# Shifted rows for the FFN moved tile by tile into two buffers, in a six-layer attention kernel

## What is computed

```python
def shift_tokens(t):
    a, s = jnp.split(t, 2, -1)
    s = jnp.pad(s, ((0, 0), (1, 0), (0, 0)))[:, :-1]
    return jnp.concatenate([a, s], -1)
...
def ffn_layer(x, g, bln, W1, b1, W2, b2):
    mu = x.mean(-1, keepdims=True)
    var = ((x - mu) ** 2).mean(-1, keepdims=True)
    xn = (x - mu) / jnp.sqrt(var + 1e-05) * g + bln
    hg = xn @ W1 + b1
    a, gate = jnp.split(hg, 2, -1)
    return a * jax.nn.gelu(gate, approximate=False) @ W2 + b2
...
for i in range(DEPTH):
    x = attn_layer(shift_tokens(x), Wqkv[i], q_scale[i], k_scale[i], Wo[i]) + x
    x = ffn_layer(shift_tokens(x), ln_g[i], ln_b[i], W1[i], b1[i], W2[i], b2[i]) + x
```

## Time and profile before

| | |
|---|---|
| median of 3 runs | 2215.2 us (2207.94 to 2216.47) |
| the profiled execution | 2216.56 us |
| its span in the trace | 2214.5 us |
| busy: TensorE / VectorE / ScalarE / GpSimd | 86% / 69% / 58% / 66% of the span |
| mean granted TensorE clock | 0.938 |
| transfers into `behind` | 48 instructions, 24 of line 218 and 24 of line 219 |

### The profile page before, as it was taken

The page is one execution under the profiler, slowest core; times in us unless marked ns, Lnnn a source line. Parts: engine busy times, 40 slices in busy tenths (PEclk is TensorE's granted clock), DMA queues, the critical chain, the costliest instruction groups (busy, mean ns, idle before and its releaser), DMA issues.

```text
span 2214.5 us, 61533 instructions
## 1 busy us (share of the span) xinstructions
PE 1898.6 (86%) x24771; PEld 1306.2 (59%) x24771; DVE 1528.6 (69%) x2364; ACT 1293.0 (58%) x1860; POOL 1472.5 (66%) x2112
## 2 busy tenths in 40 slices
PE   5789999968789988899889888898889888898885
PEld 2455555545566666566666566566666666566663
DVE  2445454458777787787777867787677876787872
ACT  3567777535556655565656655565556655565552
POOL 3344444458778677787777867787677776787771
PEclk8899999988999999999999999999899998999998
DMA  4999999920020000110000200002000020000000
GB/s 122 307 349 355 340 360 345 323 58 9 11 60 11 11 13 11 47 23 11 12 11 21 52 11 12 11 10 62 10 11 13 10 61 11 12 10 12 13 9 22
DMA packets 109618, 175.05 MB, mean 79 GB/s; under 512 B 49517, under 2 KB 72985, under 8 KB 108569
## 3 DMA queue, kind: packets, MB, share of 16 engines
q1 hardware_dynamic: 109336, 171.11, 24.9%
HBM read 87.06 MB, written 68.29 MB: 70 GB/s over the span
## 4 chain that ended last, share of the span: by engine, by line
PE 33%; DVE 17%; issue 11%; DMA 11%; POOL 4%; ACT 2%; SPq 1%; DVEq 0%; POOLq 0%; ACTq 0%
DMA behind<-x 10%; DVE turned L703 7%; PE yps L610 6%; PE ring L594 6%; PE ring L629 6%; PE ring L580 5%; PE ring L535 4%; PE ring L545 4%; DVE rsum L739 2%; DVE smax L724 2%; DVE pT L752 2%; DVE ss L718 1%; ACT squares L378 1%; POOL roped L328 1%; DVE stats L768 1%
## 5 line engine op out<-in xcount | busy, mean ns | idle before, releaser
L703 DVE TENSOR_TENSOR turned<-ring,ropes 128x1024 f32<-128x1024 f32 x384 | 447.5, 1207 | 20.4 <-PE ring L535 19.8
L610 PEld LDWEIGHTS yps<-wvo,oT 128*128 128x128 f32 x3072 | 398.4, 207 | 53.2 <-issue 50.0
L610 PE MATMUL yps<-wvo,oT 128*128 128x128 f32 x3072 | 405.6, 289 | 2.8 <-issue 2.1
L535 PE MATMUL ring<-wqk,xT 128*128 128x512 f32 x768 | 368.2, 602 | 7.7 <-issue 3.7
L328 POOL TENSOR_TENSOR roped<-roped,rnorm 128x1024 f32<-128x1024 f32 x192 | 362.3, 1902 | 7.5
L244 POOL TENSOR_TENSOR roped<-turned 128x512 f32<-128x512 f32 x288 | 357.5, 1271 | 13.3 <-DVE turned L703 13.3
L378 ACT ACTIVATE squares<-ring 128x1024 f32<-128x1024 f32 x192 | 197.5, 1029 | 268.8 <-DVE turned L703 268.0
L545 PE MATMUL ring<-ident,roped 128*128 128x128 f32 x1536 | 218.6, 292 | 146.0 <-ACT squares L378 128.7
L1233 POOL TENSOR_SCALAR less<-less,lowest 128x512 f32<-128x512 f32 x256 | 174.4, 693 | 241.1 <-DVE lowest L1202 241.1
L545 PEld LDWEIGHTS ring<-ident,roped 128*128 128x128 f32 x1536 | 187.9, 151 | 224.3 <-POOL roped L328 159.8
L1202 DVE CUSTOM_DVE_ANT_0 less<-ps_b,shifted 128x512 f32<-128x512 f32 x256 | 166.6, 689 | 222.4 <-PE ps_b L1065 80.0
(11 more groups left out here) (136 smaller groups left out, 3017.4 us busy)
## 6 DMA issues: line engine op xcount, KB each, us to landing
shifted<-scratch_w SPq DMA_DIRECT2D x64, 1024.0 KB, 12.7
scratch_w<-wrows SPq DMA_DIRECT2D x48, 1026.0 KB, 11.0
scratch_w<-x SPq DMA_DIRECT2D x16, 1026.0 KB, 10.3
wqk<-in_l_wqkv SPq DMA_DIRECT2D x6, 1024.0 KB, 5.4
xs<-xs SPq DMA_DIRECT2D x96, 48.0 KB, 1.9
wv<-in_l_wqkv SPq DMA_DIRECT2D x6, 512.0 KB
wo<-in_l_wo SPq DMA_DIRECT2D x24, 128.0 KB
xs<-x SPq DMA_DIRECT2D x96, 32.0 KB
```

Source lines behind the costliest of these rows:

```text
L535: last = nc.tensor.matmul(out[:, half, :], xT[:, t % SEQT * P:(t % SEQT + 1) * P], wqk[:, layer_of(t), at + half * 512:at + (half + 1) * 5 ...
L610: last = nc.tensor.matmul(out[:, 0:D], oT[:, h, :], wvo[:, layer_of(t), r, j, :], start=h == 0, stop=h == HEADS - 1)
L703: ins = nc.vector.tensor_tensor(turned[:, n, part, :].rearrange("p (h d) -> p h d", d=DH), heads, table, ALU.mult)
```

## The change

The four tiles of a group are moved one by one. In step `n`, after `windows(n)`, SyncE now issues the transfers of tile `n - 3`: first the single row that comes from the tile before (not for a group's first tile), then, behind `y_added` of this very tile, the 127 rows. `behind` has two buffers, used by the groups in turn, and the guard against overwriting it looks one group further back. The statistics wait for 7 transfers per group instead of 2.

```diff
-        behind = sb("behind", [P, SEQT, D // 2])
+        behind = sb("behind", [P, 2, SEQT, D // 2])
...
-        OWN, PREV, LOADS, BEHIND = 3 * 16, 2 * 16, 10 * 16, 2 * 16
+        OWN, PREV, LOADS, BEHIND = 3 * 16, 2 * 16, 10 * 16, (2 * SEQT - 1) * 16
...
-            return x[:, g % BATCH * SEQT + tile, 0:half], behind[:, tile, :]
+            return x[:, g % BATCH * SEQT + tile, 0:half], behind[:, g % 2, tile, :]
...
-            def shift(g):
-
-                at, half = g % BATCH * SEQT, D // 2
-                sp.wait_ge(s["y_added"], SEQT * (g + 1))
-                at_least(sp, s["xn_made"], g)
-                sp.dma_start(behind[1:P, :, :], x[0:P - 1, at:at + SEQT, half:D]).then_inc(s["behind_in"], 16)
-                sp.dma_start(behind[0:1, 1:SEQT, :], x[P - 1:P, at:at + SEQT - 1, half:D]).then_inc(s["behind_in"], 16)
+            def shift(t):
+
+                if live(t):
+                    at, tile, half, p = t % TILES, t % SEQT, D // 2, t // SEQT % 2
+                    at_least(sp, s["xn_made"], t // SEQT - 1)
+                    if tile > 0:
+                        sp.dma_start(behind[0:1, p, tile, :], x[P - 1:P, at - 1, half:D]).then_inc(s["behind_in"], 16)
+                    sp.wait_ge(s["y_added"], t + 1)
+                    sp.dma_start(behind[1:P, p, tile, :], x[0:P - 1, at, half:D]).then_inc(s["behind_in"], 16)
...
                 windows(n)
-                if n % SEQT == 2 and n >= SEQT:
-                    shift(n // SEQT - 1)
+                shift(n - 3)
                 if n % (SEQT * BATCH) == 10 and n // (SEQT * BATCH) + 1 < DEPTH:
                     load_layer(n // (SEQT * BATCH) + 1)
-            for g in range(GROUPS - 1, GROUPS):
-                shift(g)
+            for t in range(NT - 3, NT):
+                shift(t)
...
-            nc.gpsimd.memset(behind[0:1, 0, :], 0.0).then_inc(s["cleared"], 1)
+            nc.gpsimd.memset(behind[0:1, :, 0, :], 0.0).then_inc(s["cleared"], 1)
```

## The result

| | before | changed |
|---|---|---|
| median of the runs | 2214.12 us (2207.94 to 2216.47) | 2025.36 us (2022.62 to 2026.38) |
| the profiled execution | 2216.56 us | 2026.38 us |
| its span in the trace | 2214.5 us | 2024.3 us |
| mean granted TensorE clock | 0.938 | 0.974 |

The ratio is 0.9149, 95% interval [0.9128, 0.9171]. The change is faster by 189 us; 165 were forecast (2049 us), and the range ended at 2032. The way and the mechanism were forecast, the size was not: 24 us more came out.

What follows compares the result with a forecast made beforehand. Bound: VectorE's wait before `stats` for the transfer into `behind`, stalling all engines. Plain stretches 140.5, value-weight stretches 24.8 and last group 6.6, less 4.6 new waits, give 167.3 us; 2216.56 becomes 2049 us, range 2032 to 2088.

Steps and rivals of the forecast that it cites:

- What bounds the kernel: VectorE's wait before `stats` for the transfer into `behind`, 171.9 us in total, with TensorE and GpSimd idle and TensorE's clock lowered.
- the late tile: Fourth tile's 127 rows, issued after its own `add_y`, land within 3.68 us; at most 0.75 of 7.46 us wait stays.
- VectorE's wait: Sign: the wait before `stats`, once per group, falls from 171.9 us in total to under 25.
- SyncE's 7 us: Sign: the 7.00 us that the second transfer instruction held SyncE behind the 508-row one are gone.
- TensorE's wait for the squares: Sign: TensorE's idle time until ScalarE's squares let it turn q, 5.93 us in one stretch, is nearly gone.
- The plain stretches: 18 stretches from one `smax` to the next, 423.09 us together, shrink to 15.7 each; gain 140.5 us.
- The five stretches with value weights: Stretches where the next layer's value weights are multiplied, 128.33 us together, shrink to 20.7 each; gain 24.8 us.
- The new waits: Thin margins on VectorE, TensorE and GpSimd cost 0.2 us for each of 23 stretches, 4.6 us in total.
- the fixed time: Rival: a transfer's time is fixed, so 127 rows come as late as 508 and nothing changes; 2217 us, 3%.
- The transfer that lands later than the windows' copy: Rival: the fourth tile's copy meets others on the queue and takes 5.5 us; 31 us less gain, 2080 us, 9%.
- SyncE as the bound: Rival: added instructions each hold the queue 7.00 us, making a SyncE step 19.4 us; slower, 2450 us, 2%.
- The rule weighed against the change: Skill page's general DMA cost: 127 KB lands 2.3 us after issue, 31.75 KB 2.07, so splitting gains 0.2 us a group.

Runs made afterwards that it cites:

- the pairs: Changed kernel, but tiles moved two at a time, 254 rows behind every second tile's add_y; 2073.72 us, ratio 0.9377.
- the cut at 112: Changed kernel with each 127-row copy into `behind` cut into 112 and 15 partitions; 2020.39 us in the first set, 2016.84 in the second.

## Why the prediction was too small

*What bounds the kernel, and the late tile:* right. VectorE's wait fell to 18.4 us (under 25 expected), the transfer landed after 3.74 us (3.68), SyncE's 7 us are gone, and TensorE's wait for the squares fell from 128.7 us to 3.0.

*The plain stretches:* right, 139.95 us against 140.5. The reason given for 15.7 us was half wrong. I had TensorE as their bound; TensorE idles 0.45 us there (15.52 less 15.07 in the stretch above) while VectorE stands 0.83 us, and the pairs show that each further microsecond of VectorE's wait is felt in full. With the cut at 112 the 18 stretches sum to 275.97 us, 0.4 us less each, and there TensorE is the bound. VectorE's work and wait together (14.59 and 0.83) come within half a microsecond of TensorE's 15.07, so 15.7 fits either bound; that the number held is in part luck.

*The five stretches with value weights:* this is the step that failed: "TensorE idles 3.55 before the turns and loses 3.02 − 1.95 = 1.07 to the clock: 20.63 stay". The loss to the clock was read on one group of instructions only. The value weights' products between the two, 3.78 us at 1.2 GHz and 2.06 at 2.4, lost another 1.72. With it 18.91 stay; measured were 18.47 to 18.90. The term is 35.35 us, not 24.8. The trace of before held the price only at the low clock, 3.55 to 3.79 us in all five places, and I took it for the work's own. It could have told that this is the price at 1.2 GHz: ahead of the first layer the same products took 3.79 us in a stretch with a granted clock of 0.50:

```profile
473.18 3.79 PE L566 MATMUL ring<-wo,wvT 64*128 64x128 f32 x32 [0.98 <-ACT wvT L437]
...
472.90:478.00 5.10, 4.82 (x34) 4.13 (x35) 0.00 (x0) 2.56 (x6) 0.00 (x0) 0.50 0.09 21
```

A stretch with a granted clock of 0.86 should have been searched for every instruction in it, and these products given bounds of half the time, 1.89 us, and 3.78.

*The new waits, 4.6 us:* they did not come. The plain stretches' 15.7 held with the remaining wait in it.

*The five stretches ahead of those, 7.2 us:* not forecast. They contain no statistics, and TensorE idles there for GpSimd's `roped` before and after. Two of the five ran at a granted clock of 1.00 in the changed kernel and took 14.98 and 15.36 us; none did before, at 0.82 to 0.90 with 16.54 to 20.31 us. Why the clock held there in some and not in others was not tried and stays open.

The sum of what the steps missed, 10.5 + 4.6 + 7.2, is 22.3 of the 22.9 us by which the profiled executions' difference (190.2) exceeds 167.3. The range was too narrow at its lower end because the five stretches had no bounds of their own.

*The rivals:* the fixed time fell with the pairs. The transfer that lands later than the windows' copy and SyncE as the bound did not occur. The rule weighed against the change, the fixed 2.0 us plus bytes over 436e3 per us of the Trainium skill, "DMA: Bandwidth & Descriptors", section "Anatomy of one DMA", fitted there for transfers that GpSimd issues, does not describe these copies, which took 3.74, 6.03 and 10.38 us. But the other way out of the same wait, one transfer in a better shape, I did not see: 2030.9 us with all of the old order.

## What to carry to other kernels

When an engine waits long for a small copy, look at the copy's shape before its place: here 127 partitions cost 10.38 us where 112 and 15 cost 3.62, and moving work earlier only hid what a cut removes. When a stall is to go, price every instruction behind it at the clock that it will have, not at the one in the trace: a granted clock below 1.00 in a stretch means that some of its prices may not be the work's own. When several engines stand in the same stall, forecast the next bound from each one's busy time in the stretch, and check which of them keeps a wait.

## What the runs showed of the hardware

A copy between partitions of the on-chip memory over 127 partitions took 17 to 18 ns for each further row of 256 bytes: from issue to the reader 3.74 us for 127 rows, 6.03 for 254 and 10.38 for 511. The same 511 rows cut at 112 partitions took 3.62 us. An instruction behind such a copy on SyncE was held the longer the more rows it had, though not in proportion: in the groups shown above 0.81 us behind 127 rows, 2.73 behind 254, 5.07 behind 381 and 7.00 behind 508, against 0.96 and 0.76 behind the two that were cut. TensorE's float32 product of 128x128x128 took 0.227 us, where a turn of the same size took 0.13, both at a granted clock of 1.00.
